# Two halves written out, with most of the modulation computed at the end of causal attention

## The chip, the cores and the metric

The kernel runs on one core of one Trainium2 chip, as one program. The metric is the device time of one execution in microseconds; of the kernel before there are three timed runs and one profiled execution. In the rows, PE is TensorE (PEld its weight loads), DVE VectorE, ACT ScalarE, POOL GpSimd and SP SyncE, which here only issues DMAs; a name with a q behind it is that engine's queue. Times are in us unless marked otherwise.

## The reference

Two transformer layers with adaptive layer norm, in float32, on x of 4 batches, 512 tokens and 512 features. Cut to what matters:

```python
mod = (silu(c) @ wmod).reshape(4, 6, 1, 512)            # per layer: sa, ca, ga, sb, cb, gb
ga = (2 * (ga >= 0) - 1) * maximum(abs(ga), 0.25)       # the gates; gb alike
h = layernorm(x) * (1 + ca) + sa
x = x + ga * causal_attention(h)    # layer 0: 32 query heads, 8 key/value heads of 128, rotary, wo
h = layernorm(x) * (1 + cb) + sb
x = x + gb * sign_ffn(h)            # sign(W), scaled by row_scale = mean|W| of a row, and scale_param
mod = (silu(c1) @ wmod1) ...        # layer 1, with its own c and wmod
x = x + ga * head_attention(h)      # layer 1: 32 heads of 16, attention among the heads of one token
x = x + gb * lora_experts(h)        # 8 experts of rank 16, the best one is chosen
```

`wmod0` and `wmod1` are 512 x 3072 each, 6 MB; one sixth of one of them, 512 x 512 and 1 MB, gives one of the six vectors per layer and is called a chunk here.

## The kernel before

**Stages.** Every stage is a block in which each engine has its own list of instructions, written out by hand and tied by semaphores; at its end stands a barrier of all engines (L81). A stage's work starts when the slowest engine, and the last DMA that SP waits for, are done.

1. `stage_modulation` (L90 to L203), once: SP loads both wmods in eight parts, PE multiplies silu(c) by them with the 4 batch columns as weights and 512 columns moving (L157), ACT takes the 4x512 rows out (L144), PE turns eight of the twelve into columns (L167) for `modT`, DVE makes the four gates (L190 to L196) and the mean of |W| (L182); gates and row_scale go to DRAM.
2. Then a loop on the device (`nc.Fori`) runs twice, over the two halves of the batches (2 batches, 1024 tokens each). In each pass: `stage_half_mod` copies this half's two columns of `modT` to `modh` (L497). `stage_norm` loads x and the gates (L370, L331), clears y, normalises batch by batch (statistics L413, Newton steps L433 to L436, `xn` L438), turns xn on PE (L459), applies scale and shift on ACT (L481), and splits the result, and the first group's weights, into a high part `hh` and a low part `hl` (L447, L392, L450; weights L534 and L538).
3. `stage_groups` (causal attention) runs once per half, in 64 steps, one for a query head and a batch; n counts them. Step n on PE: transposes of the probabilities (L732), the projection of a later query or key (L690), scores of head n + 1 (L715), `out_proj` for an earlier head pair (L771), and `weigh(n)`, probabilities times values (L753); ACT takes the product out (L876). The last steps have no projection. Behind step 63 stand four more output tiles. Weights come in eight groups; SP loads the next group's when POOL has split the last (L516, L521), and behind group 7 it loads group 0's again. `pj` is the PSUM bank most projections use; a projection waits until the bank's last one was taken by DVE.
4. `stage_middle`: residual, second norm, sign product, residual, third norm. `stage_qkv`: projections of layer 1, stored to DRAM in another order.
5. `stage_heads_and_finish` ("tail"): 16 pieces (`CHUNKS`) of attention among heads, whose first keys lie in the memory of y (`kd0`); gathers of the result by SP and ACT (L1468); output projection (L1526); last norm, experts (L1541, L1555); stores of x (L1491), for which SP waits.

## Time and profile before

| | us |
|---|---|
| timed runs | 2323.23, 2324.77, 2325.0 (median 2324.77) |
| the profiled execution, its own time | 2326.28 |
| span of its trace | 2324.4 |
| PE busy | 2038.9 |
| DVE, ACT, POOL busy | 1472.6, 1054.6, 1045.4 |
| mean granted clock of PE | 0.94 |

The span runs from the first to the last instruction in the trace; 1.9 us of the time lie around it. A row of a timeline gives start, duration, engine, line, operation, output and inputs, and in brackets how long the engine was idle before it and what ended that.

### The profile page before, as it was taken

To read this page: it belongs to the slowest core of one execution; us is meant where nothing else is said; L and a number is where in the kernel's file an instruction comes from. 1 tells how busy PE (TensorE), PEld (TensorE's weight loads), DVE (VectorE), ACT (ScalarE), POOL (GpSimd) and SP (SyncE) were. 2 spreads that over 40 slices of the span, in tenths; PEclk is the share of its full clock that TensorE was granted. 3 is DMA by queue.
4 is the path that set the end of the run, shared out by engine and by line. 5 is a ranking of instruction groups with operands and counts; after the bars stand their busy time and mean duration, and the time that the engine had idled before them with its cause. 6 is when DMAs were issued, how large, how long until landed. Compare 5 with 4: busy or idle time off the path is not lost. (4 is left out here: it accounts for less than half of the span.)

```text
span 2324.4 us, 34095 instructions
## 1 busy us (share of the span) xinstructions
PE 2038.9 (88%) x11760; PEld 1636.0 (70%) x11760; DVE 1472.6 (63%) x3703; ACT 1054.6 (45%) x2426; POOL 1045.4 (45%) x818
## 2 busy tenths in 40 slices
PE   7389999999999996587846999999999999964887
PEld 1278888888888885276525888888888888733664
DVE  1666666666666667833765666666666666676176
ACT  1255555555555553324214555555555555532232
POOL 0354555455555553343126545556455454435141
PEclk9599999999999998798977999999999999977989
DMA  6300000010000103025330001000010100030371
GB/s 250 118 19 28 19 28 19 28 46 19 28 19 28 46 19 120 12 73 118 70 128 28 19 28 46 19 28 19 28 39 13 41 19 28 19 132 28 94 128 47
DMA packets 129763, 118.55 MB, mean 51 GB/s; under 512 B 43172, under 2 KB 95396, under 8 KB 128564
## 3 DMA queue, kind: packets, MB, share of 16 engines
q1 hardware_dynamic: 121332, 107.07, 15.6%
q10 hardware_dynamic: 8256, 9.25, 1.4%
q8 instruction: 97, 1.59, 0.3%
q14 instruction: 78, 0.64, 0.1%
HBM read 95.29 MB, written 16.81 MB: 48 GB/s over the span
## 5 line engine op out<-in xcount | busy, mean ns | idle before, releaser
L996 POOL TENSOR_TENSOR gqa_rot<-gqa_rot,consts 128x512 f32<-128x512 f32 x160 | 209.4, 1309 | 641.9 <-ACT gqa_rot L817 641.8
L833 ACT ACTIVATE gqa_prob<-gqa_prob,gqa_nmax 128x128 f32<-128x128 f32 (+3 forms) x512 | 281.9, 552 | 198.5 <-DVE gqa_nmax L918 198.5
L918 DVE CUSTOM_DVE_ANT_0 gqa_prob<-gqa_pS,consts 128x128 f32<-128x128 f32 (+3 forms) x512 | 220.2, 486 | 73.8 <-PE gqa_pS L717 72.9
L926 DVE TENSOR_TENSOR gqa_ptl<-gqa_pT,gqa_pth 128x384 fp32r<-128x384 f32 (+1 forms) x384 | 218.2, 596 | 32.0 <-ACT gqa_pth L843 27.3
L843 ACT CAST gqa_pth<-gqa_pT 128x384 fp32r<-128x384 f32 (+1 forms) x384 | 182.5, 510 | 94.5 <-PE gqa_pT L732 94.5
L999 POOL TENSOR_TENSOR gqa_full<-gqa_full,gqa_rot 128x512 f32<-128x512 f32 x160 | 206.5, 1291 | 12.6
L771 PE MATMUL gqa_pW<-woh,gqa_oh 128*128 128x512 f32 x504 | 202.7, 402 | 9.0 <-DVE y L943 9.0
L690 PE MATMUL gqa_pj<-first_hh,wqh 128*128 128x512 f32 x496 | 205.7, 415 | 0.0
L771 PE MATMUL gqa_pW<-woh,gqa_ol 128*128 128x512 f32 x504 | 197.3, 392 | 0.0
L1008 POOL TENSOR_TENSOR gqa_ql<-gqa_full,gqa_qh 128x512 fp32r<-128x512 f32 x128 | 164.3, 1283 | 73.0 <-DVE gqa_qh L907 73.0
L771 PE MATMUL gqa_pW<-wol,gqa_oh 128*128 128x512 f32 x504 | 196.5, 390 | 0.0
L690 PE MATMUL gqa_pj<-first_hh,wql 128*128 128x512 f32 x496 | 194.5, 392 | 0.0
L690 PE MATMUL gqa_pj<-first_hl,wqh 128*128 128x512 f32 x496 | 193.6, 390 | 0.0
L715 PE MATMUL gqa_pS<-gqa_kh,gqa_qh 128*128 128x192 f32 (+3 forms) x512 | 172.5, 337 | 18.0 <-POOL gqa_ql L1008 17.7
L732 PE MATMUL gqa_pT<-consts,gqa_prob 128*128 128x128 f32 x1280 | 182.9, 274 | 2.1 <-DVE gqa_ptl L926 2.1
L876 ACT CAST gqa_oh<-gqa_pO 128x512 fp32r<-128x512 f32 x128 | 75.1, 587 | 239.7 <-PE gqa_pO L753 239.7
L732 PEld LDWEIGHTS gqa_pT<-consts,gqa_prob 128*128 128x128 f32 x1280 | 156.0, 141 | 36.1 <-DVE gqa_ptl L926 3.0
L935 DVE TENSOR_SCALAR gqa_prob<-gqa_prob,gqa_rden 128x128 f32<-128x128 f32 (+3 forms) x512 | 178.2, 411 | 4.5
L753 PE MATMUL gqa_pO<-gqa_pth,gqa_vh 128*128 128x512 f32 (+3 forms) x512 | 167.1, 326 | 14.7 <-DVE gqa_ptl L926 14.7
L943 DVE TENSOR_TENSOR y<-gqa_pW,y 128x512 f32<-128x512 f32 x252 | 171.7, 681 | 8.5 <-PE gqa_pW L771 5.6
L889 DVE SCALAR_TENSOR_TENSOR gqa_full<-gqa_pj,consts 128x512 f32<-128x512 f32 x156 | 107.4, 688 | 99.1 <-ACT gqa_rot L817 92.5
L717 PE MATMUL gqa_pS<-gqa_kh,gqa_ql 128*128 128x192 f32 (+3 forms) x512 | 165.7, 324 | 0.0
(245 smaller groups left out, 4866.8 us busy)
## 6 DMA issues: line engine op xcount, KB each, us to landing
raw_q<-in_wq SPq DMA_DIRECT2D x16, 1024.0 KB, 5.3
raw_o<-in_wo SPq DMA_DIRECT2D x16, 1024.0 KB, 5.2
mod_wm<-in_wmod SPq DMA_DIRECT2D x8, 1536.0 KB, 19.4
raw_kv<-in_wkv SPq DMA_DIRECT2D x16, 512.0 KB, 6.6
x<-in_x SPq DMA_DIRECT2D x4, 1024.0 KB, 6.4
kp<-qkv_rest SPq DMA_DIRECT2D x16, 256.0 KB, 2.3
qp<-qkv_rest SPq DMA_DIRECT2D x16, 256.0 KB, 2.3
vp<-qkv_rest SPq DMA_DIRECT2D x64, 64.0 KB, 1.8
```

Source lines behind the costliest of these rows:

```text
L690: mm = pe.matmul(bank[e][:], wp, hp[:, k, t], start=(n == 0), stop=(n == 3 * KT - 1))
L715: pe.matmul(out, qh[r][:, t], kh[u % 2][:, 0:wide], start=True, stop=False)
L732: mm = pe.transpose(pT[k % 2][:, c:c + P], prob[n % 2][:, P_OFF[i] + j * P:P_OFF[i] + (j + 1) * P], held.ident)
L771: mm = pe.matmul(wbank(d)[:], op[h % 4][:, t], wp[:, h % R0, :], start=(m == 0), stop=(m == 5))
L833: ins = nc.scalar.activation(p, p, ACT.Exp, scale=-1.0, bias=nmax[r][:, i:i + 1], accum_out=den[r][:, i:i + 1])
L843: nc.scalar.copy(pth[:, c:c + w], pT[k % 2][:, 0:w]).then_inc(pt_hi, 1)
L918: nc.vector.tensor_tensor_reduce(prob[r][:, P_OFF[i]:P_OFF[i] + w], pS[s][:, c:c + w], held.mask[:, T - w:T], -1.0, LARGEST, ALU.add, ALU.min,
L926: nc.vector.tensor_tensor(ptl[:, c:c + w], pT[k % 2][:, 0:w], pth[:, c:c + w].bitcast(F32), ALU.subtract).then_inc(pt_lo, 1)
L935: ins = nc.vector.tensor_scalar(p, p, rden[n % 2][:, i:i + 1], None, ALU.mult)
L943: nc.vector.tensor_tensor(y[:, j, :], wbank(d)[:], y[:, j, :], ALU.add).then_inc(w_added, 1)
L996: nc.gpsimd.tensor_tensor(rot[r % 2][:], rot[r % 2][:], held.sinT, ALU.mult).then_inc(sined, 1)
L999: nc.gpsimd.tensor_tensor(full[r % 2][:], full[r % 2][:], rot[r % 2][:], ALU.add).then_inc(roped, 1)
```

## The change

The loop over the halves is written out, so each stage exists twice, with constants where registers were; `stage_half_mod` and `modh`'s copy are gone (`modh` is a slice of `modT`). `stage_modulation` is gone. In `stage_first` of half 1, x and two chunks (shift and scale of the first norm) are loaded, PE computes the two between the two batches' transposes, with 128x128 pieces of wmod as weights and the 4 batch columns moving, so that columns come out directly. x lies in memory for half 2 already: it is loaded into y's memory in half 1's last stage, and x and y change places. y is cleared by POOL instead of DVE, and the Newton step has one operation less. raw_o is loaded in attention instead of in the norm.

The other ten chunks are computed in half 1's attention: nine behind `weigh(n)` of steps 55 to 63 and one behind step 63, each loaded by SP into the memory of raw_q when the chunk before is computed, each taken out by DVE. The gates, turned on PE, go to DRAM from there, and so does row_scale (`sign_scale`). Group 0's weights are no longer loaded and split behind group 7.

```diff
-def stage_modulation(nc, held, a):
...
-        with nc.Block() as block:
...
-                for l in range(2):
-                    for k in range(KT):
-                        pe.wait_ge(wm_in[l][k], 16)
-                        for i in range(NCH):
-                            if l and k == 0:
-                                pe.wait_ge(row_out, i + 1)
-                            mm = pe.matmul(pr[i][:], silu[:, k, l * B:(l + 1) * B], wm[l][:, k, i * D:(i + 1) * D],
-                                           start=(k == 0), stop=(k == KT - 1))
...
+def stage_first(nc, held, a, half, weights):
...
+            pM = [pT[HB * KT - 2 + i][:, 0:KT * B].rearrange("p (m b) -> p m b", b=B) for i in range(2)]
...
+                if half == 0:
+                    for l, c in enumerate((a["c0T"], a["c1T"])):
+                        sp.dma_start(cT[:, :, l * B:(l + 1) * B], c.rearrange("(k p) b -> p k b", p=P)).then_inc(c_in, 16)
+                    load_x(sp, 0)
+                    for i in range(2):
+                        sp.dma_start(wm[i][:], a["wmod0"][:, i * D:(i + 1) * D].rearrange("(k p) n -> p k n", p=P)).then_inc(wm_in[i], 16)
+                    load_x(sp, 1)
+                    rest = slice(0, 2 * T)
+                    sp.dma_start(held.consts[:, rest], a["tables"][:, rest]).then_inc(const_in, 16)
+                    sp.wait_ge(const_in, 16)
...
+                nc.gpsimd.memset(y[:], 0.0).then_inc(y_clear, 1)
+                def weight_los():
                     for n, (what, i) in enumerate(FIRST_PARTS):
                         pool.wait_ge(split_hi, n + 1)
                         weights.split_lo(what, i).then_inc(split_lo, 1)
-                if ahead:
-                    ahead.los(pool)
+
...
+                    v, h, r, t = var[:, s], half_var[:, s], rstd[:, s], step[:, s]
                     link(nc.vector.tensor_scalar(v, mv[:, s, 1], EPS, None, ALU.add))
+                    nc.vector.tensor_scalar(h, v, -0.5, None, ALU.mult)
...
-                        link(nc.vector.tensor_tensor(t, t, v, ALU.mult))
-                        link(nc.vector.tensor_scalar(t, t, -0.5, 1.5, ALU.mult, ALU.add))
-                        link(nc.vector.tensor_tensor(r, r, t, ALU.mult))
+                        link(nc.vector.tensor_tensor(t, t, h, ALU.mult))
+                        link(nc.vector.scalar_tensor_tensor(r, t, 1.5, r, ALU.add, ALU.mult))
...
+                normalise(0)
+                if half == 0:
+                    for ci in range(2):
+                        dve.wait_ge(mod_full, ci + 1)
+                        nc.vector.tensor_scalar(held.modT[:, 0, ci], pM[ci], float(ci), None, ALU.add).then_inc(mod_done, 1)
+                normalise(1)
...
+                turn(0)
+                if half == 0:
+                    for i in range(2):
+                        pe.wait_ge(wm_in[i], 16)
+                        for m in range(KT):
+                            for k in range(KT):
+                                mm = pe.matmul(pM[i][:, m, :], wm[i][:, k, m * P:(m + 1) * P], held.silu[:, k, 0:B],
+                                               start=(k == 0), stop=(k == KT - 1))
+                        mm.then_inc(mod_full, 1)
+                    pe.wait_ge(mod_done, 2)
+                turn(1)
...
+                if half == 0:
+                    ident = slice(2 * T, held.consts.shape[1])
+                    act.dma_start(held.consts[:, ident], a["tables"][:, ident]).then_inc(ident_in, 16)
+                    act.wait_ge(c_in, 32)
+                    nc.scalar.activation(ec[:], cT[:], ACT.Exp, scale=-1.0).then_inc(c_exp, 1)
+                    act.wait_ge(wm_in[0], 16)
+                weights.load_qkv(act, w_in, 0)
+
+                def weight_his():
+                    act.wait_ge(w_in, 32)
                     for what, i in FIRST_PARTS:
                         weights.split_hi(what, i).then_inc(split_hi, 1)
-                if ahead:
-                    ahead.load(act)
-                    for loaded in later:
...
-def stage_half_mod(nc, held, half):
...
-    for gr in range(GB):
+    for gr in range(GB - 1):
...
+LATER = [(0, 2), (0, 5), (1, 2), (1, 5), (0, 3), (0, 4), (1, 0), (1, 1), (1, 3), (1, 4)]
+NGATE = 4
+LATER_AT = 55
+STEP_OF = [0] * 4 + [n for n, step in enumerate(STEP_PROJ) for e in step]
...
+                wts.load_o(sp, wo_in, 0)
+                if later:
+                    sp.dma_start(sp_scale[:], a["scale_param"]).then_inc(sign_in, 16)
+                else:
+                    load_gates(sp, held, a, 0, half, gate_in)
+                for i in range(GB - 1):
                     if i:
                         sp.wait_ge(w_lo, last_split(("q", "kv"), i))
-                    wts.load_qkv(sp, qkv_in, after[i])
+                    wts.load_qkv(sp, qkv_in, i + 1)
                     sp.wait_ge(w_lo, last_split(("o",), i))
-                    wts.load_o(sp, wo_in, after[i])
+                    wts.load_o(sp, wo_in, i + 1)
+                sp.wait_ge(w_lo, last_split(("q", "kv"), GB - 1))
+                for j, (l, c) in enumerate(later):
+                    if j == 6:
+                        sp.wait_ge(w_lo, last_split(("o",), GB - 1))
+                        sp.dma_start(wts.raw_o[:], a["w_sign"].rearrange("(k p) n -> p k n", p=P)).then_inc(sign_in, 16)
+                    if j:
+                        sp.wait_ge(chunk_full, j)
+                    sp.dma_start(wts.raw_q[:], a["wmod0" if l == 0 else "wmod1"][:, c * D:(c + 1) * D].rearrange("(k p) n -> p k n", p=P)
+                                 ).then_inc(chunk_in, 16)
+                    if j == 6:
+                        sp.wait_ge(gate_left, 1)
+                        sp.dma_start(a["gates"].rearrange("g b (m p) -> (g b m) p", p=P), grow[:]).then_inc(rows_out, 16)
+                if later:
+                    sp.wait_ge(rows_out, 16)
+                    load_gates(sp, held, a, 0, half, gate_in)
+                    sp.wait_ge(scale_step, 3)
+                    sp.dma_start(a["row_scale"].rearrange("(k p) -> p k", p=P), row_scale[:], allow_slow_non_contiguous=True).then_inc(rows_out, 16)
+                    sp.wait_ge(rows_out, 32)
...
+                    if later and STEP_OF[e] > LATER_AT:
+                        pe.wait_ge(chunk_left, STEP_OF[e] - LATER_AT)
...
+                def modulate(j):
+
+                    n = LATER_AT + j
+                    free(max(e for e in range(len(PROJ)) if bank[e] is pj and STEP_OF[e] <= n))
+                    if j:
+                        pe.wait_ge(chunk_left, j)
+                    if j == NGATE:
+                        pe.wait_ge(gate_step, 5)
+                        pe.transpose(pj[0:NGATE * B * KT, T - P:], gT[:].rearrange("p g b m -> p (g b m)"), held.ident).then_inc(gate_turned, 1)
+                    pe.wait_ge(chunk_in, 16 * (j + 1))
+                    for m in range(KT):
+                        for k in range(KT):
+                            mm = pe.matmul(pj[:, m * B:(m + 1) * B], wts.raw_q[:, k, m * P:(m + 1) * P],
+                                           held.silu[:, k, later[j][0] * B:(later[j][0] + 1) * B], start=(k == 0), stop=(k == KT - 1))
+                    mm.then_inc(chunk_full, 1)
...
+                    if 0 <= n - LATER_AT < len(later):
+                        modulate(n - LATER_AT)
                     if n >= 2:
                         out_proj(2 * (n - 2) + 1)
+                for j in range(NH - LATER_AT, len(later)):
+                    modulate(j)
...
+                def modulation(j):
+
+                    l, c = later[j]
+                    dve.wait_ge(chunk_full, j + 1)
+                    got = pj[:, 0:KT * B].rearrange("p (m b) -> p m b", b=B)
+                    if j == NGATE:
+                        dve.wait_ge(gate_turned, 1)
+                        nc.vector.tensor_copy(grow[:], pj[0:NGATE * B * KT, T - P:]).then_inc(gate_left, 1)
+                    if j < NGATE:
+                        nc.vector.tensor_copy(gT[:, j].rearrange("p b m -> p m b"), got).then_inc(chunk_left, 1)
+                    else:
+                        ci = (0, 1, 3, 4).index(c)
+                        nc.vector.tensor_scalar(held.modT[:, l, ci], got, float(ci % 2), None, ALU.add).then_inc(chunk_left, 1)
+                    if j == NGATE - 1:
...
+                def sign_scale():
+
+                    dve.wait_ge(sign_in, 32)
+                    nc.vector.tensor_reduce(row_scale[:], wts.raw_o[:], AX.X, ALU.add, apply_absolute_value=True).then_inc(scale_step, 1)
...
+                for j in range(NH - LATER_AT, len(later)):
+                    modulation(j)
+                if later:
+                    sign_scale()
...
+                if half + 1 < B // HB:
+                    sp.wait_ge(s_full, CU * (UNITS1 - NK // 2))
+                    for b in range(HB):
+                        t0 = (half + 1) * HB * T + b * T
+                        sp.dma_start(held.y[:, b * TT:(b + 1) * TT, :], a["x"][t0:t0 + T, :].rearrange("(j p) d -> p j d", p=P)
+                                     ).then_inc(next_in, 16)
...
-        with nc.Fori(0, B // HB) as half:
-            stage_half_mod(nc, held, half)
+        for half in range(B // HB):
+            held.modh = held.modT[:, :, :, :, half * HB:(half + 1) * HB]
...
-                    stage_norm(nc, held, a, 0, 0, half, weights=wts)
-                    with nc.Fori(0, G // GB) as g:
-                        stage_groups(nc, held, a, wts, g * GB)
+                    wts = GroupWeights(gctx, nc, a, half)
+                    stage_first(nc, held, a, half, wts)
...
+            held.x, held.y = held.y, held.x
```

## Rows read from the trace of the kernel before

**Rows 1.** Profile page, busy time by engine over the span.
```profile
PE 2038.9 (88%) x11760; PEld 1636.0 (70%) x11760; DVE 1472.6 (63%) x3703; ACT 1054.6 (45%) x2426; POOL 1045.4 (45%) x818
```

**Rows 2.** Attention by stretch: us; busy PE, PEld, DVE, ACT, POOL; PEclk; DMA share; GB/s.
```profile
205.00:305.00 100.00, 98.57 (x529) 83.96 (x528) 66.68 (x179) 54.12 (x134) 51.38 (x40) 1.00 0.09 27
```

**Rows 3.** Timeline, modulation stage: start, duration, engine, line, output and input, count.
```profile
9.86 43.80 PE L157 MATMUL mod_pr<-mod_wm,mod_silu 128*4 128x512 f32 x96 [9.86 <-DMA mod_wm<-in_wmod]
...
38.71 2.29 DVE L182 TENSOR_REDUCE mod_rs<-mod_w 128x4 f32<-128x2048 f32 x1 [31.34 <-DMA mod_sp<-in_scale_param]
...
53.59 2.04 PEld L167 LDWEIGHTS mod_pc<-consts,mod_row 4*128 4x128 f32 x32 [0.86 <-issue]
```

**Rows 4.** Timeline, half-modulation copy, first norm and start of attention, half 1.
```profile
66.08 0.20 DVE L497 COPY modh<-modT 128x64 f32 x1 [3.01 <-PEq L81]
...
72.53 2.47 DVE L413 BATCH_NORM_STATS2 ln_stats<-x 128x6 f32<-128x512 f32 x4 [1.17 <-DMA x<-in_x]
...
78.31 1.92 DVE L438 TENSOR_SCALAR ln_xn<-x,ln_mv,ln_rstd 128x512 f32<-128x512 f32 x4
...
85.91 4.78 DVE L438 TENSOR_SCALAR ln_xn<-x,ln_mv,ln_rstd 128x512 f32<-128x512 f32 x4
...
104.26 0.76 PE L690 MATMUL gqa_pj<-first_hh,wkvh 128*128 128x512 f32 x1 [12.40 <-PEq L81]
```

**Rows 5.** Timeline of SyncE's DMA issues at the end of half 1.
```profile
1190.87 0.33 SPq L1491 DMA_DIRECT2D out<-x  x1
```

**Rows 6.** Timeline, from the last store of half 1 to half 2's norm.
```profile
1197.78 0.19 DVE L497 COPY modh<-modT 128x64 f32 x1 [8.43 <-issue]
...
1204.03 2.47 DVE L413 BATCH_NORM_STATS2 ln_stats<-x 128x6 f32<-128x512 f32 x4 [0.97 <-DMA x<-in_x]
...
1231.46 3.41 DVE L450 TENSOR_TENSOR first_hl<-ln_hf,first_hh 128x512 fp32r<-128x512 f32 x2
```

**Rows 7.** Timeline, a run of eight small products in the last stage.
```profile
1167.36 1.00 PEld L1541 LDWEIGHTS tail_pS<-lora_wA,tail_hf 128*128 128x128 f32 x8
```

**Rows 8.** The list of DMA issues from the trace, the output stores.
```profile
out<-x SPq DMA_DIRECT2D x16, 256.0 KB, 2.0
```

**Rows 9.** Timeline, end of attention and start of the middle stage.
```profile
901.79 0.47 PE L771 MATMUL gqa_pW<-woh,gqa_oh 128*128 128x512 f32 x1 [0.88 <-DVE y L943]
...
907.53 0.69 DVE L943 TENSOR_TENSOR y<-gqa_pO,y 128x512 f32<-128x512 f32 x1 [0.67 <-PE gqa_pO L771]
...
909.28 0.69 DVE L1115 TENSOR_TENSOR y<-y,gate 128x512 f32<-128x512 f32 x1 [1.06 <-PEq L81]
```

**Rows 10.** Timeline, GpSimd clearing a tile as large as y.
```profile
1007.14 3.53 POOL L1337 MEMSET y<- 128x4096 f32 x1
```

**Rows 11.** Profile page, DMA issues: transfer, count, size, median us to landing.
```profile
raw_q<-in_wq SPq DMA_DIRECT2D x16, 1024.0 KB, 5.3
```

**Rows 12.** Timeline, ScalarE taking each head's output, steps 54 and 55.
```profile
800.37 0.59 ACT L876 CAST gqa_oh<-gqa_pO 128x512 fp32r<-128x512 f32 x1 [1.31 <-PE gqa_pO L753]
...
811.02 0.59 ACT L876 CAST gqa_oh<-gqa_pO 128x512 fp32r<-128x512 f32 x1 [2.04 <-PE gqa_pO L753]
```

**Rows 13.** Timeline of SyncE's DMA issues, after the splits of step 54.
```profile
803.71 0.37 SPq L516 DMA_DIRECT2D raw_q<-in_wq  x1
```

**Rows 14.** Timeline, ScalarE taking the outputs of steps 62 and 63.
```profile
892.47 0.59 ACT L876 CAST gqa_oh<-gqa_pO 128x512 fp32r<-128x512 f32 x1 [2.65 <-PE gqa_pO L753]
...
899.54 0.59 ACT L876 CAST gqa_oh<-gqa_pO 128x512 fp32r<-128x512 f32 x1 [2.80 <-PE gqa_pO L753]
```

**Rows 15.** Timeline, PE after its idle time in half 1's last stage.
```profile
1183.69 0.69 PE L1549 MATMUL tail_pG<-consts,tail_wt 128*128 128x128 f32 x2 [4.28 <-DVE tail_wt L1745]
```

**Rows 16.** Table by stretch (columns as in Rows 2), the same place.
```profile
1182.00:1184.00 2.00, 0.31 (x2) 0.29 (x2) 1.50 (x7) 0.00 (x0) 0.39 (x1) 0.54 0.66 248
```

**Rows 17.** Timeline, last stage: SyncE's gathers.
```profile
1118.12 18.54 SPq L1468 DMA_DIRECT2D tail_at<-tail_o  x24
```

**Rows 18.** Timeline, last stage: PE's first output projections.
```profile
1130.52 10.57 PE L1526 MATMUL tail_pG<-out_w,tail_at 128*128 128x512 f32 x24
```

453 lines of the change are left out of this document (180 added, 273 removed).

## The prediction, made before the change was run

> **What bounds the kernel now.** I read the page's busy shares first: PE is busy for 88% of the span [rows 1]. A share over the whole span mixes stages, so the table by stretch came next. Inside causal attention, two stages of some 800 us each, PE is busy 98.57 of 100 us at a granted clock of 1.00 [rows 2], that is 2.4 GHz. Work put on PE there is paid in full; work on DVE (67%), ACT (54%) or POOL (51%) is not. Then I read the timelines of the places the change touches. In front of everything stands the modulation stage, where PE works through 96 records of 128x512 from 9.86 us for 43.8 us [rows 3]; the code has 48 matmuls there (2 layers, 4 k, 6 chunks), so **a float32 matmul makes two records**. DVE's gate and column work follows, and the next stage starts at 66.08 [rows 4]. The first norm's statistics start at 72.53 and the first attention matmul at 104.26 [rows 4]. So 104 us pass before the bound engine does work that bounds. Between the halves, the last store is issued at 1190.87 [rows 5] and the next norm's statistics start at 1204.03 [rows 6], with PE idle.
>
> **The change, part by part.** All times are from the profiled execution: span 2324.4, its own time 2326.3, which is 1.5 above the median of the runs shown (2324.8). I sum against 2326.3 and take the 1.5 off at the end.
>
> *Front of half 1.* The new first stage needs x's first MB, wmod0's first two chunks (1 MB each) and x's second MB, in this order on SP's queue. Transfer speed: the tables (0.8 MB) and the first wmod part (1.5 MB) had landed when PE started at 9.86 [rows 3], so with about 2 us to the first byte they moved at about 0.3 MB/us or better. Estimates: x's first MB by 7.5, chunk 1 by about 14, x's second MB by about 22, with attention's first weights on ScalarE's queue beside it. Statistics to xn took 78.31 - 72.53 = 5.8; the Newton step loses three linked operations of 0.2, so 5.3, and xn takes 1.92 [rows 4]: 14.7. PE's transposes end about 16. Then 2 chunks of 16 matmuls, 64 records. **Price of a record** of 128 weight columns and 4 moving columns: before has none. The nearest row is the transposition of 4-row slices, also 128 weight columns and 4 moving columns: 32 in 2.04 us, 0.064 each [rows 3]. The other end is a product with a full 128x128 weight tile and 136 moving columns: 8 in 1.00, 0.125 each [rows 7]. Less than 0.064 I exclude only down to 0.05, since nothing in the trace with 128 weight columns is quicker. I take 0.064, as the moving size is the same, and near twice that for part of the front, where PE has just begun: 6 us, to 22, and DVE's two additions to 22.5. The second norm: 2.5 + 2.9 on DVE, but now POOL works on hl and the weight splits beside it. Four tensor_scalars of xn took 4.78 beside POOL against 1.92 alone [rows 4]; I put 1.5 on Newton's four and take 4.8 for xn: 34. From the end of xn (85.91 + 4.78 = 90.69) to the first attention matmul passed 13.6 [rows 4]; ScalarE and POOL now have six splits each on that path or beside it, but POOL's end before the second half of it, so I take 12.5: attention starts at 46.5. Gain 104.3 - 46.5 = **57.8** (52 to 62).
>
> *Between the halves.* The last store lands 2.0 after its issue [rows 8], at 1192.9; with a barrier of 1.0 (DVE's last addition ends at 908.2, the next stage's first work stands at 909.3 [rows 9]) a stage that follows at once starts at 1193.9. Before, the copy of the half's modulation only started at 1197.78 [rows 6]: 3.9 for the loop's way back, which goes. The copy's own stage, the load of x and the clearing of y by DVE fill the rest to 1204.03, and go too, since x lies there and POOL clears y (3.53 [rows 10]). Sum 10.1. Inside the stage (1204.03 to 1234.87 [rows 6]) the Newton steps give 1.0, but weight splits on POOL now start some 5 us earlier and fall on the second Newton step: I take 1.5 net (-1 to 4). Gain **11.6**. The copy at 66.08 and its stage lie in the first term.
>
> *Loads in front of attention.* raw_o is loaded at the start of attention (5.3 [rows 11]) and needed at step 0's end, some 30 us on; in half 2 SP also waits for the gates before the next group's load, which has two steps of 10.7 us (811.02 - 800.37 [rows 12]) and more: 0. The last group's six splits per half go from ACT and POOL, which have slack: 0.
>
> *Ten chunks at the end of attention, half 1.* Each is 32 records at 0.064 = 2.05 on the engine that is busy all the time: 10 x 2.05 = **+20.5** (at 0.125: +40). Are their weights there in time? SP issued the load behind step 54's splits at 803.71 [rows 13], 1 MB takes 5.3 [rows 11], so 809.0; step 55's product ends at 810.8, just before ACT takes it [rows 12]. Cover 1.8, so chunk 0 waits for nothing. Chunks 1 to 7 are loaded from the end of the last chunk, with a step of 10.7 or more for 5.4. Chunk 8 has 7.1 (899.54 - 892.47 [rows 14]) plus its own 2: hidden. PE's waits added before projections (chunk_left) are met by a DVE copy that stands ahead of the addition, while PE runs an output projection of 1.4; behind such a wait the whole of PE would stand. **Chunk 9 has no step left.** Let T be the end of step 63's product, 899.4. Chunk 8 ends at T + 2.1, the load lands at T + 7.6, PE's only other work is one output projection (to T + 3.5). The last tiles, which began at 901.79 = T + 2.4 [rows 9], now start at T + 9.7: +7.3, of which 4.1 are the two chunks already counted, so **+3.2**. DVE then does sign_scale before the additions: the reduction of 2.29 [rows 3] and two small ones, 2.9, and PE's third tile waits for the first addition: **+1.0**. SP's gates and row_scale transfers end before the additions: 0. **Clock**: in half 1's last stage PE was idle for 4.28 before 1183.69 [rows 15], and the granted clock was 0.54 in 1182 to 1184 [rows 16], near 1.2 GHz. An idle stretch of 4.1 before chunk 9 is of that size. At 1.2 GHz the last chunk and some tiles take twice as long: **+2.5** (0 to 7).
>
> By the Trainium skill, "TensorE: Matmul & The Clock Gate", LDWEIGHTS, loading P weight columns takes P/1.2 ns, 107 ns for 128, whatever the rows. The row of 0.064 [rows 3] speaks against it; by the page the ten chunks would be 34 and the whole sum 14 us longer.
>
> *x for half 2 in the last stage.* SP issued its gathers from 1118.12 [rows 17]; the two x loads stand ahead of them, 1 us of issuing, and 2 MB ahead in the same queue, some 9 to 10 us. PE's first output projection was at 1130.52 [rows 18], so the first gather lands about then: **+0.5** (0 to 3).
>
> Sum: -57.8 - 11.6 + 20.5 + 3.2 + 1.0 + 2.5 + 0.5 = -41.7. 2326.3 - 41.7 = 2284.6, less 1.5: **2283**.
>
> **The rivals.**
> *Dense weights cost more.* If a record costs 0.107 to 0.125, the ten chunks take 34 to 40 instead of 20.5 and the front 1 to 2 more: 2298 to 2305. For it: the dense product's row [rows 7]; against: there the moving 136 columns may be what takes the time. Chance 0.25. This is also what the skill's rule gives.
> *Front shorter.* If POOL disturbs DVE less (xn 1.92, Newton undisturbed, casts short) and the clock stays at the end, 6 + 2.5 + 2 go: 2272. Chance 0.12.
> *PE's clock falls in steps 55 to 63.* A chunk is 2 us of records in which 4 columns move. If they count as idleness and the granted clock falls to 1.2 GHz for these steps, each microsecond is doubled: the 99 us from 800.37 to 899.54 [rows 12, 14] would cost 99 more, 2382, slower than before. It decides once more than 42 of these us run at the low level. Against it: over 8 of 10 us in each step are the same dense matmuls as now, at 1.00 [rows 2]. Chance 0.03.
> *The change brings nothing in front*, because the transfers, not PE's 96 records, set the start: then x or the chunks would arrive after 40 us. The tables and 1.5 MB had landed at 9.86 [rows 3], and 4.3 MB are needed: chance below 0.01.
>
> **How the numbers follow.** Likeliest (0.58): 2283, own range 2275 to 2292. Dense weights 0.25, front shorter 0.12, clock 0.03, the rest 0.02 is spread. The range reaches over the first three: 2270 to 2305. A measurement tells about 0.2% (4.6 us) from no change; only the clock rival and half of the rest are not faster: faster 0.96, same 0.01, slower 0.03.
>
> **What would show it.** In the profile after: first attention matmul at 46.5 (42 to 52); chunk records 2.05 a chunk in steps 55 to 63 and PE's share there still near 98%; PE idle 4 us before the last chunk, released by a DMA, with a clock near 0.5 behind it; attention of half 1 longer by 27; bn_stats of half 2 about 3 us after the last store's issue. Wrong would be: a chunk that waits for its weights in steps 55 to 62, 4 us a chunk instead of 2, or a first projection of half 1's last stage that waits for a gather by more than 3 us.

## The result, and the profile after the change

| | before | after |
|---|---|---|
| time, median (lowest to highest) | 2323.4 us (2321.0 to 2326.9, 20 runs) | 2328.5 us (2319.7 to 2334.9, 20 runs) |
| after over before | | 1.002, 95% interval 1.0013 to 1.0027 |
| the profiled execution: time, span | 2326.3, 2324.4 us | 2321.9, 2320.1 us |
| first attention matmul of half 1 | 104.26 | 55.06 |
| attention of half 1, to the middle stage's first work | 805.0 | 858.7 |
| from there to the first attention matmul of half 2 | 326.5 | 317.6 |
| the rest | 1088.6 | 1088.8 |

Forecast were 2283 us and a range of 2270 to 2305; the change brought nothing: after is some 5 us slower, 0.2%, and the interval lies just above 1. (The prediction knew three runs of before, with a median of 2324.8; the 20 runs have 2323.4.) The front gave 49.2 us and the boundary of the halves 8.9 (326.5 - 317.6), and the attention of half 1 took 53.7 of them back. The profiled execution of after lies 6.6 us below its own median, and after's runs spread over 15 us where before's spread over 6; that calls for an explanation too.

The page gives little away: PE is busy for 88% of a span that is 4 us shorter [against rows 1], and its clock line, tenths of full speed in 40 slices of 58 us, is lower in slices 15, 16 and 18 than before's. Lines of the page of after, and then the clock line of before:

```profile
PE 2048.0 (88%) x12017; PEld 1683.2 (73%) x12017; DVE 1463.7 (63%) x3696; ACT 1042.1 (45%) x2402; POOL 1035.3 (45%) x808
...
PEclk6999999999999987888978999999999999977989
```

```profile
PEclk9599999999999998798977999999999999977989
```

The timelines show where the time went. In front (start, duration, engine, line, output and input, count, idle time before and who ended it), the answer to [rows 4]:

```profile
15.10 3.65 PE L386 MATMUL ln_pT<-consts,ln_xn 128*128 128x128 f32 x16 [15.10 <-DVE ln_xn L356]
18.54 10.54 PE L399 MATMUL ln_pT<-silu,ln_wm 128*128 128x4 f32 x64
...
55.06 0.76 PE L623 MATMUL gqa_pj<-first_hh,wkvh 128*128 128x512 f32 x1 [6.70 <-PEq L81]
```

```profile
9.17 2.47 DVE L341 BATCH_NORM_STATS2 ln_stats<-x 128x6 f32<-128x512 f32 x4 [3.52 <-DMA x<-in_x]
...
32.67 0.16 DVE L352 TENSOR_TENSOR ln_step<-ln_rstd 128x4 f32<-128x4 f32 x1
32.87 1.18 DVE L353 TENSOR_TENSOR ln_step<-ln_step,ln_half_var 128x4 f32<-128x4 f32 x1
...
42.64 3.77 DVE L356 TENSOR_SCALAR ln_xn<-x,ln_mv,ln_rstd 128x512 f32<-128x512 f32 x4
```

The 64 records of two chunks took 10.54 us (0.165 each) where 6 were forecast. VectorE's small operations on 128x4 elements are 0.16 us long at 32.67 and 1.18 from 32.87 on, when GpSimd's subtractions run beside them (its first starts at 32.76).

The end of attention: PE's chunks (first, fourth, last), the matmul of an output tile behind the seventh chunk, and ScalarE taking the output of heads 53 and 63, which answers to [rows 12, 14]:

```profile
761.70 3.65 PE L720 MATMUL gqa_pj<-silu,raw_q 128*128 128x4 f32 x32
...
809.69 3.65 PE L720 MATMUL gqa_pj<-silu,raw_q 128*128 128x4 f32 x32
...
860.99 0.77 PE L704 MATMUL gqa_pW<-woh,gqa_oh 128*128 128x512 f32 x1
...
893.91 6.96 PE L720 MATMUL gqa_pj<-silu,raw_q 128*128 128x4 f32 x32 [3.76 <-DMA raw_q<-in_wmod]
```

```profile
737.08 0.59 ACT L830 CAST gqa_oh<-gqa_pO 128x512 fp32r<-128x512 f32 x1 [1.83 <-PE gqa_pO L686]
...
885.14 0.59 ACT L830 CAST gqa_oh<-gqa_pO 128x512 fp32r<-128x512 f32 x1 [2.82 <-PE gqa_pO L686]
```

A chunk takes 3.65 us, not 2.05; the next matmul starts 3.51 behind a chunk's first of 32 records, 0.110 a record. The output tile at 860.99 is at half pace (the next matmul of the same form follows 0.57 later and then every 0.43, where 0.23 is the distance at full clock). The granted clock was at its lower level there, 1.2 GHz, with PE busy all the time: the table by stretch of two such places (us; busy PE, PEld, DVE, ACT, POOL with counts; PEclk; DMA share; GB/s):

```profile
843.00:847.00 4.00, 4.00 (x14) 3.31 (x15) 0.60 (x2) 0.00 (x0) 0.00 (x0) 0.50 0.49 141
859.00:863.00 4.00, 4.00 (x17) 3.61 (x17) 0.17 (x1) 0.00 (x0) 0.30 (x1) 0.52 0.16 18
```

The last chunk waits 3.76 us for its weights and then takes 6.96 us. Behind it, VectorE's reduction, the store of row_scale and the middle stage's first work, the answer to [rows 9]:

```profile
901.00 2.27 DVE L926 TENSOR_REDUCE gqa_row_scale<-raw_o 128x4 f32<-128x2048 f32 x1
...
913.74 1.79 DVE L1108 TENSOR_TENSOR y<-y,gate 128x512 f32<-128x512 f32 x1 [5.23 <-PEq L81]
```

```profile
903.76 0.37 SPq L587 DMA_DIRECT2D row_scale<-gqa_row_scale  x1
913.71 0.38 SPq L102 DMA_DIRECT2D mid_hf<-in_w_signT  x1
```

```profile
row_scale<-gqa_row_scale SPq DMA_DIRECT2D x1, 2.0 KB, 8.9
```

VectorE stood idle for 5.23 us in front of the middle stage instead of 1.06: SyncE had issued the store of row_scale, 512 single 4-byte elements, at 903.76; it landed 8.9 us later, and the barrier follows.

**Split of the 53.7 us.** Until ScalarE takes head 53's output (786.2 before, 737.1 after) both kernels need the same time from the first attention matmul: 682.0 in both. In before:

```profile
786.22 0.59 ACT L876 CAST gqa_oh<-gqa_pO 128x512 fp32r<-128x512 f32 x1 [1.81 <-PE gqa_pO L753]
```

All of the difference lies behind it. From there to head 63's output (ten steps, called the ten steps from here on) there are 113.3 us before and 148.0 after (+34.7, eight chunks); from there to the last addition's start 8.0 and 22.7 (+14.7, two chunks and the reduction); from there to the middle stage 1.75 and 5.9 (+4.2). The table by stretch, before and then after, for the ten steps:

```profile
786.20:899.50 113.30, 108.60 (x589) 92.42 (x590) 75.31 (x199) 59.13 (x146) 52.24 (x41) 1.00 0.08 24
```

```profile
737.10:885.10 148.00, 145.36 (x847) 129.23 (x848) 78.03 (x213) 56.34 (x140) 44.37 (x35) 0.93 0.22 72
```

A mean granted clock of 0.93 over 148.0 us is a loss of some 10.4 us against full clock (an estimate, 148.0 x 0.07); without it the steps would have taken 137.6, so eight chunks cost 24.3, or 3.0 each. That is less than 8 x 3.51: PE was idle 4.7 us in before's ten steps and 2.6 in after's, and the rest of the difference is open. That gives the first theory: **work 24.3, clock 10.4, in the ten steps**. Its rivals: the loads or waits of the chunks, not their matmuls; and written-out code that runs slower than a loop.

### The profile page after: what moved, and what is told of

Read it like the earlier page. It is cut to its first block and busy times, and to the rows that moved or that the text cites. A ratio compares the mean times of both kernels' runs of the same rounds, so it can differ in the third digit from the quotient of the medians.

```text
span 2320.1 us, 34359 instructions
## 1 busy us (share of the span) xinstructions
PE 2048.0 (88%) x12017; PEld 1683.2 (73%) x12017; DVE 1463.7 (63%) x3696; ACT 1042.1 (45%) x2402; POOL 1035.3 (45%) x808
## 5 line engine op out<-in xcount | busy, mean ns | idle before, releaser
L992 POOL TENSOR_TENSOR gqa_full<-gqa_full,gqa_rot 128x512 f32<-128x512 f32 x160 | 206.6, 1291 | 12.6
L648 PE MATMUL gqa_pS<-gqa_kh,gqa_qh 128*128 128x192 f32 (+3 forms) x512 | 173.2, 338 | 16.4 <-POOL gqa_ql L1001 16.0
L686 PE MATMUL gqa_pO<-gqa_pth,gqa_vl 128*128 128x512 f32 (+3 forms) x512 | 165.6, 323 | 0.0
```

Of the source, the lines that this page charges most:

```text
L648: pe.matmul(out, qh[r][:, t], kh[u % 2][:, 0:wide], start=True, stop=False)
L686: mm = pe.matmul(pO[:, T - w:], vp[u % 2][:, v], pp[:, pc], start=(m == 0), stop=(m == 11))
L992: nc.gpsimd.tensor_tensor(full[r % 2][:], full[r % 2][:], rot[r % 2][:], ALU.add).then_inc(roped, 1)
```

## The experiments

Medians are compared with after's 2328.5. The kernel before was timed again beside each group of experiments, with medians of 2323.4 to 2325.0, so differences of 1 or 2 us between experiments say nothing. Each kernel is named by its label; the diffs are abridged.

**e1_one: the chunks' matmuls taken out.** Of 16 matmuls of a chunk one is left; the chunk values, and with them the gates and modulations, are not computed.

```diff
-for m in range(KT):
-    for k in range(KT):
-        mm = pe.matmul(pj[:, m*B:(m+1)*B], wts.raw_q[:, k, m*P:(m+1)*P], held.silu[...], ...)
+mm = pe.matmul(pj[:, 0:KT*B], wts.raw_q[:, 0, 0:P], held.ident[:, 0:KT*B], start=True, stop=True)
```

> Each of the ten chunks is computed with one matmul (2 records) instead of 16 (32 records); the other 15 are left out, so the ten chunks' values are not computed (gates and modulation come out wrong). Loads, evictions, waits and order stay. Theory A (the chunks cost what their records show in the changed kernel, 3.5 us each, and pull TensorE's clock down for a few us after each): 10 x 3.3 = 33 us fewer of work, and the windows with a granted clock of 0.5 to 0.9 behind each chunk vanish, another 7 to 12 us: 40 to 45 us below the changed kernel, 2283 to 2290. Theory B (the prediction's price of 2.05 us a chunk was right and the rest of the 53.7 us of the first attention lies elsewhere): 19 us less, about 2309, with the gap between two chunks still long. Theory C (the time of the chunks is that of their loads or evictions, not of the matmuls): less than 5 us.

Measured 2280.0 (2276.9 to 2281.6): 48.4 us below after (40.3 between the profiled executions, of which after's lay low). The ten steps take 115.4 us instead of 148.0, with the clock at 1.00:

```profile
740.50:855.90 115.40, 110.58 (x608) 94.29 (x608) 78.23 (x213) 56.11 (x141) 44.67 (x35) 1.00 0.28 92
```

So the chunks' matmuls, not their loads and waits (which are all still there), cost about as much as the front gains. Theories B and C fall; A's 40 to 45 was a little low. Whether it is their work or their clock this run does not part.

**e2_wide and e8_wide8: more columns beside the same weights.** The 4 moving columns are read 24 times (8 times in e8_wide8) with a step of zero; the result's first copy is used.

```diff
-mm = pe.matmul(pj[:, m*B:(m+1)*B], wts.raw_q[:, k, m*P:(m+1)*P], silu, ...)
+mm = pe.matmul(pj[:, m*24*B:(m+1)*24*B], wts.raw_q[:, k, m*P:(m+1)*P], silu.to_broadcast([P, 24, B]), ...)
```

> Each chunk matmul gets its 4 moving columns 24 times over (96 columns, read with a step of zero), so the same weights are loaded the same number of times and the results are the same; 24 times as many columns are streamed. Theory A (the record of 0.110 us is the load of the 128x128 weights, beside which 96 columns fit, and the clock falls behind a chunk because TensorE streams almost nothing during it): a chunk stays at 3.5 to 4.0 us at full clock, the windows at 0.5 to 0.9 behind the chunks vanish, and the kernel is 5 to 12 us faster than the changed one: 2316 to 2323. Theory B (the record's time goes by columns, or the clock falls for the gap that the weight loads leave whatever is streamed): a chunk takes 6 us or more, or the clock windows stay, and the kernel is 0 to 30 us slower than the changed one.

> The chunk matmuls with their 4 columns 8 times over (32 columns a record instead of 4; with 96 it was 14 us faster than the changed kernel, a chunk at 3.7 us and no fall of the clock before the last chunks). Theory A (the granted clock follows how many columns are streamed during the chunks): a part of the falls stays, 2 to 8 us faster than the changed kernel. Theory B (it is enough that the moving operand is not tiny): the whole 14 us. Theory C (the gain of the 96-column run came from the run's own luck with the clock): no difference from the changed kernel, 2326 to 2331.

Measured 2314.3 (2309.5 to 2319.2) with 96 columns and 2317.0 (2316.3 to 2318.7) with 32. A chunk of e2_wide, and the ten steps of e2_wide and of e8_wide8:

```profile
852.28 3.73 PE L722 MATMUL gqa_pj<-silu,raw_q 128*128 128x96 f32 x32
```

```profile
737.60:876.40 138.80, 135.78 (x848) 120.95 (x848) 77.56 (x213) 56.08 (x141) 44.41 (x35) 1.00 0.23 77
```

```profile
738.10:881.70 143.60, 140.55 (x849) 125.13 (x848) 77.81 (x213) 56.21 (x141) 44.40 (x35) 0.96 0.23 74
```

24 times as many columns cost 3.73 instead of 3.65 us, so the 0.110 us of a record do not go by its columns. Nor is 0.110 what any record costs: in before, records with weights of 32 columns and 68 moving columns start 0.049 apart (32 in 1.58), and transposes of full 128x128 tiles with 128 moving columns 0.110 (4 in 0.44), both at full clock:

```profile
1097.97 1.65 PE L1518 MATMUL tail_pO<-tail_bd,tail_pt 128*32 128x68 f32 x32
1099.55 1.08 PE L1504 MATMUL tail_pS<-y,tail_qq 64*32 64x128 f32 x32
...
1162.23 0.60 PE L1534 MATMUL tail_pO<-consts,tail_xn 128*128 128x128 f32 x4
1162.67 0.60 PE L1534 MATMUL tail_pG<-consts,tail_xn 128*128 128x128 f32 x4
```

What is left is that **a record's price is the load of its 128x128 weights**. And the clock does not fall any more in the ten steps: 1.00 with 96 columns, 0.96 with 32, 0.93 with 4. The same work became 14 us faster by streaming more, a little more than theory A's 5 to 12. With 32 columns the median is 11.5 lower, between theory A's part and theory B's whole; the runs of the two kernels overlap, so it is the clock in their profiles, and not the medians, that tells 32 columns from 96.

**e11_again: after itself, a second profile.**

> The changed kernel itself once more. Its profiled run (2321.9) lies 6.6 us below its median of 2328.5, and its runs spread over 15 us where those of before spread over 6. Theory A (the spread is the granted clock in steps 56 to 63): in a new profiled run the stretch from 740 to 900 us loses another amount than the 15 us of full-speed time of the first profile (each 20 us window's missing share of the clock, summed), and the run's time moves with it, by about half to the whole of the difference; the other stages stay within 1 us. Theory B (the spread comes from loads or from the start): the clock there is as in the first profile, and another stage carries the difference.

Measured 2329.1 (2321.6 to 2333.8); this profiled execution took 2333.7, 11.7 more than the first. Its ten steps:

```profile
740.20:893.00 152.80, 150.11 (x849) 133.09 (x848) 78.10 (x213) 56.49 (x140) 44.42 (x35) 0.90 0.21 70
```

The clock's loss is 15.3 instead of 10.4, and the steps take 4.8 more. But the other places are not within 1 us, as I had expected: the first attention matmul comes 3.1 later, since the two chunks in front took 13.65 instead of 10.54, and 2.4 and 1.8 are lost behind the attention. So of 11.7 us between the two executions the ten steps hold 4.8 and the front 3.1; the cause of the rest stays open. In five profiles with 4 columns (four kernels, after twice) the ten steps' length and the clock go together:

| kernel | ten steps, us | granted clock | loss, us | rest, us |
|---|---|---|---|---|
| after | 148.0 | 0.93 | 10.4 | 137.6 |
| e11_again | 152.8 | 0.90 | 15.3 | 137.5 |
| e3_pool | 152.9 | 0.90 | 15.3 | 137.6 |
| e7_front | 159.2 | 0.86 | 22.3 | 136.9 |
| e5_ends | 165.7 | 0.84 | 26.5 | 139.2 |
| e8_wide8 (32 columns) | 143.6 | 0.96 | 5.7 | 137.9 |
| e2_wide (96 columns) | 138.8 | 1.00 | 0 | 138.8 |

(Loss = length x (1 - clock), rest = length - loss.) **The rest is one number, 137 to 139; what differs is the clock.** Three more kernels with 96 columns, described below (e9_wide_ends, e6_all, e10_four), were at 0.99, and their ten steps took 142.5 each, with w_sign's sums inside them. So four profiles with 96 columns stand at 0.99 to 1.00 and five with 4 columns at 0.84 to 0.93.

**e5_ends and e9_wide_ends: the waits at the ends.** w_sign's sums and row_scale's store are put between chunks 6 and 8, chunk 9 goes into the buffer of wo beside chunk 8, and the next half's x is loaded behind the gathers: in e5_ends with 4 columns, in e9_wide_ends with 96.

```diff
+if j == 8:
+    sp.wait_ge(scale_step, 3)
+    sp.dma_start(a["row_scale"]..., row_scale[:], ...)
-if j:
+if j and j != 9:
     sp.wait_ge(chunk_full, j)
-sp.dma_start(wts.raw_q[:], ...)
+sp.dma_start(chunk_at(j)[:], ...)
...
+if later and n == LATER_AT + 6:
+    sign_scale()
-if later:
-    sign_scale()
```

> The changed kernel with its order at three places altered: the row sums of w_sign and the store of row_scale go in between chunk 6's eviction and chunk 8's load instead of behind chunk 9; chunk 9 is loaded beside chunk 8, into the buffer of wo's last group (free once w_sign's sums are done), instead of behind chunk 8's matmuls; the next half's x is loaded behind the last stage's gathers instead of in front of them. Theory A (these are waits on the path: 4.2 us at the start of the middle stage for row_scale, 3.8 us at chunk 9, 3.1 us at the last stage's first projection): the idle time before the middle stage's first work falls from 5.2 to about 1, chunk 9 takes 3.5 instead of 7.0 us, the projection's wait goes to 0, and about 2 us more come back because TensorE stays at full clock through chunk 9: 10 to 13 us below the changed kernel, 2315 to 2319. Theory B (each gives its place to the next wait: the gates' broadcast loads behind rows_out, the clock at the end of the attention, the gathers' own time): 0 to 4 us.

> The three edits of the ends (w_sign's sums and row_scale's store early, chunk 9 in a buffer of its own, the next half's x behind the gathers) on top of the chunks with 96 columns a record. With 4 columns a record the same three edits removed their waits in the trace and yet left the median where it was, with runs from 2316 to 2334. Theory A (the clock hid them: with 4 columns every few us of idle time gained go to a deeper fall of the clock in steps 56 to 63): here the clock is steady, so they count: 10 to 13 us below the 96-column run of 2314.3, at 2301 to 2305. Theory B (they are worth nothing on the path, and the later kernel with all edits owed its gain to its front and its second half): 2310 to 2315.

e5_ends: 2327.9 (2315.9 to 2334.2), no gain in the median; its mean, 2325.0, is 3.5 below after's, which is not clear of the noise. e9_wide_ends: 2301.7 (2299.9 to 2303.3), 12.6 below e2_wide, as theory A had it. The profiled executions are 6.2 apart, as e2_wide's lay 4.8 below its median; there, 3.8 us come from the middle stage's start and 6.7 from the end of attention, and 3.7 are given back in the ten steps, where the sums now stand. The waits did go in both. The first work of the middle stage and the last stage's first projection in e5_ends, and that projection in after:

```profile
926.11 1.79 DVE L1111 TENSOR_TENSOR y<-y,gate 128x512 f32<-128x512 f32 x1 [0.94 <-PEq L81]
...
1145.34 4.99 PE L1531 MATMUL tail_pG<-out_w,tail_at 128*128 128x512 f32 x11
```

```profile
1136.86 10.57 PE L1528 MATMUL tail_pG<-out_w,tail_at 128*128 128x512 f32 x24 [3.10 <-DMA tail_at<-tail_o]
```

Idle time of 0.94 instead of 5.23 us in front of the one, none instead of 3.10 in front of the other. In e5_ends' profiled run the ten steps took 17.7 more than in after's at a clock of 0.84, which ate all of it in that execution. Its runs lie in two groups, five at 2315.9 to 2318.4 and seven at 2326.9 to 2334.2, and the profiled one is of the upper group; no profile of the lower group was taken. Why its clock fell more than after's stays open; the order of the work in the steps before chunk 6 is the same.

**e3_pool and e7_front: VectorE beside GpSimd.** In e3_pool GpSimd waits with the weight parts until the second norm's Newton steps are done (in half 2 with all but two of them); e7_front does the weight parts of half 1 first, while VectorE waits for the two chunks.

```diff
 # e3_pool, GpSimd, half 1
+pool.wait_ge(newton, HB * (3 + 3 * NEWTON))
 # e7_front, ScalarE and GpSimd: the "if half:" goes from in front of weight_his() and weight_los()
-if half:
-    weight_los()
+weight_los()
```

> In the changed kernel GpSimd splits the first group's weights (six 128x512 subtractions) at the same time as VectorE works through the second norm's 18 small operations. Here GpSimd waits until those are done (in the second half after the first two parts). Theory A (the two engines take turns at a shared port, and each small operation waits out one of GpSimd's): the small operations fall from 1.18 us to about 0.16 to 0.25, 7 to 9 us in each half; GpSimd's own six subtractions then start later but end before the first group's projections need them, so the kernel is 10 to 18 us faster than the changed one: 2310 to 2318. Theory B (the small operations are slow for another reason, or the weight parts become the last thing the first projection waits for): 0 to 3 us, or the first projection waits for the weights' low parts by 5 us or more and the gain is gone.

> In the first half the six weight parts are rounded and split before the first norm's own tiles on ScalarE and GpSimd (as the changed kernel has it in the second half), so they run while TensorE works on the two chunks in front and VectorE waits, and not beside the second norm's small operations. Theory A (these operations run at 1.19 us beside a GpSimd subtraction and at 0.16 without one): only the four subtractions of the first image's low parts are left beside them, about 5 of the 9 slow operations become fast, 4 to 7 us less up to the first attention matmul. Theory B (the collision moves: the normalisation of 3.8 us or the casts slow down instead, as where GpSimd was made to wait and only 2.8 us of 9 came through): 0 to 3 us. The landing of wq's and wkv's first group at about 23 us is the mark to watch: beyond 29 it would delay the first image's tiles.

e3_pool: 2322.8 (2313.8 to 2326.0), 5.7 less, between theory A's 10 to 18 and theory B's 0 to 3; e7_front: 2329.8 (2316.6 to 2335.3), no gain in the median. VectorE in e3_pool:

```profile
32.87 0.16 DVE L358 SCALAR_TENSOR_TENSOR ln_rstd<-ln_step,ln_rstd 128x4 f32<-128x4 f32 x1
...
34.26 5.83 DVE L360 TENSOR_SCALAR ln_xn<-x,ln_mv,ln_rstd 128x512 f32<-128x512 f32 x4
...
42.11 4.82 DVE L378 CAST first_hh<-ln_hf 128x512 fp32r<-128x512 f32 x4 [2.02 <-ACT ln_hf L432]
```

Each small operation is back at 0.16 us and the Newton steps end 8.4 us earlier (34.26 instead of 42.64), but now xn takes 5.83 instead of 3.77 and the casts 4.82, since the same GpSimd work lies beside them: the first attention matmul comes at 52.27, 2.8 earlier, as theory B had it; between the halves 5.6 were left. e7_front moves the work where VectorE has nothing to do: 53.10, against 58.14 of e11_again, whose chunks in front took the same 13.65: 5.0, as theory A had it. Its median shows nothing of it, for the ten steps ran at 0.86.

**e4_unrolled: before, with its two loops written out.** Only the loop statements and the buffers' names change (for half in range(B // HB) instead of nc.Fori).

> The kernel before with its two loops (over the halves and over the groups of the last stage) written out, and nothing else changed. Theory A (the loop's way back costs the 3.9 us that the trace of before shows at the boundary, and nothing in the steps): 3 to 6 us faster than before, 2317 to 2320. Theory B (written-out code costs instruction loading in every step, more than the loops' way back saves): 0 to 10 us slower than before; the attention of the first half would then be longer than its 805.0 us by about as much.

Measured 2320.1 (2317.7 to 2322.5), 3.3 below before. The copy of the half's modulation, which in [rows 6] had 8.43 us of idle time before it:

```profile
1192.07 0.20 DVE L501 COPY modh<-modT 128x64 f32<-128x64 f32 x1 [4.53 <-PEq L85]
```

3.9 us less, and the attention of half 1 is as long as before's (804.1 us to 805.0). So the way back costs what was read from it, and code written out shows no cost of its own: the other rival falls.

**e6_all and e10_four: the better version.** e6_all has 96 columns, the three edits of the ends, the early weight parts and GpSimd's wait in half 2; e10_four also computes the second norm's two chunks in the front, one before and one behind the second image's transposes, and needs chunk 9's own buffer no more.

> All of these together: 96 columns a record in the chunks, w_sign's sums and row_scale's store early, chunk 9 in a buffer of its own, the next half's x behind the gathers, the weight parts early in the first half, and GpSimd waiting for the small operations in the second half. By the single runs: 14 (columns) + 10 to 13 (ends, less the 2 us that both count) + 4 (front) + 3 (second half) = 29 to 32 us below the changed kernel, 2296 to 2300. If each wait only makes room for the next: 2305 to 2314.

> The kernel of all edits (2292.9) with two of the ten chunks, the second norm's modulation, brought to the front: one in TensorE's idle time before the second image's transposes, one behind them, each beside work of VectorE and ScalarE; eight chunks stay in the attention, and w_sign's sums stay early. Theory A (TensorE is idle 10 us and 7 us there, and a chunk takes 3.7 to 6.8 us): the front stays within 1 us and the attention is 2 x 3.7 us shorter: 7 us below, 2285 to 2287; if TensorE also starts the projections at full pace because it was busy before them, another 2 to 4 us. Theory B (at the half pace of the front a chunk takes 6.8 us, and its 1 MB of loads comes in with the first group's): the front grows by 3 to 8 us and the kernel stays at 2290 to 2296.

e6_all: 2292.9 (2288.7 to 2296.3), ratio to before 0.986 (0.985 to 0.988), 3 us below the least that the single runs added up to. e10_four: **2288.2** (2286.6 to 2290.9), ratio 0.985 (0.983 to 0.987), 40 us below after, and between theory A's 2285 to 2287 and theory B's 2290 to 2296. The two ratios' intervals overlap, so that e10_four is the faster of the two is not shown. The front of e10_four, PE, and GpSimd's first weight part in e10_four and in e6_all:

```profile
18.79 10.54 PE L405 MATMUL ln_pT<-silu,ln_wm 128*128 128x4 f32 x64
...
34.56 6.96 PE L405 MATMUL ln_pT<-silu,ln_wm 128*128 128x4 f32 x32 [5.23 <-issue]
43.02 3.62 PE L394 MATMUL ln_pT<-consts,ln_xn 128*128 128x128 f32 x16 [1.50 <-DVE ln_xn L357]
...
46.47 3.73 PE L405 MATMUL ln_pT<-silu,ln_wm 128*128 128x4 f32 x32
...
53.43 0.77 PE L636 MATMUL gqa_pj<-first_hh,wkvh 128*128 128x512 f32 x1 [3.22 <-PEq L81]
```

```profile
29.26 1.27 POOL L255 TENSOR_TENSOR wkvl<-raw_kv,wkvh 128x512 fp32r<-128x512 f32 x1 [25.01 <-ACT wkvh L251]
```

```profile
24.24 1.27 POOL L255 TENSOR_TENSOR wkvl<-raw_kv,wkvh 128x512 fp32r<-128x512 f32 x1 [19.99 <-ACT wkvh L251]
```

Theory B holds for the front, where attention starts 3.4 later than in e6_all (50.07). The third chunk did run at half pace, 6.96, but the second image's transposes did not wait for it: it was done at 41.5, and they waited 1.50 more for VectorE's xn, which started at 42.42 instead of 39.12. Two more MB are loaded beside the first group's weights, and ScalarE got those at 28.6 instead of 23.5; so GpSimd's weight parts start 5 us later and fall on more of VectorE's small operations, the collision of e3_pool once more. Theory A holds for the end: from head 63's output to the last addition 8.0 us, as before the change, instead of 14.0.

## Why the prediction was wrong

The sum in the profiled execution should have been 2284.6 and was 2321.9: 37.3 us. The other 8.1 us between 2283 and 2328.5 are that the profiled execution of before was taken as 1.5 above its median and after's lay 6.6 below its own.

- **The price of a record, the step that failed.** The prediction had two rows, 0.064 [rows 3] and 0.125 [rows 7], and chose the first because its moving size was the same, 4 columns. The moving size did not matter: with 96 columns a chunk costs the same but for 0.08 us (e2_wide). The weights differed, 4 partitions deep in the row of 0.064 and full tiles of 128 partitions in the row of 0.125, and full tiles measured 0.110 at full clock. The row of 0.064 is also one of transposes, but transposes of full tiles start 0.110 apart as well; that the 4 partitions make it cheap is what is left, and no run changed them alone. By the Trainium skill, "TensorE: Matmul & The Clock Gate", LDWEIGHTS, 128 weight columns take 107 ns, and the prediction set this aside because of the row of 0.064; for full tiles this trace agrees with it (0.110), and for weights of 4 partitions the row still speaks against it. The 14 us that the prediction put on this rule left out the front's 64 records, some 3 us by the same figures (an estimate from the 107 ns of that page of the Trainium skill). Eight chunks cost 24.3 instead of 16.4: 7.9 of the 37.3.
- **The clock in steps 55 to 63, in the sum at nothing and a rival at 0.03; this step failed too, and by more.** The prediction argued that 8 of 10 us in a step are dense. That was no reason: the granted clock fell behind chunks (0.50 in 843 to 847, 0.52 in 859 to 863), for a few us, not for the whole of the steps. So the size of 99 us was wrong and so was the zero: 10.4 us in the profiled run and 15 to 27 in others. Of the 11.7 us between two executions of after, 4.8 lie in the ten steps. Why the clock fell: e2_wide and e8_wide8 change nothing but the number of streamed columns, and it rose with them.
- **The end of attention**: forecast +10.8 (two chunks 4.1, wait 3.2, sign_scale 1.0, clock 2.5), measured +14.7. The wait of chunk 9 was right (3.76 idle, released by the DMA), and the half clock behind it too; but at the true price of a record the chunk took 6.96 there.
- **row_scale: forecast 0, measured +4.2.** The prediction had the store end before the additions. It is issued behind the reduction, at 903.76, and landed 8.9 us later; the prediction gave 512 single elements of 4 bytes no time of their own. e5_ends and e9_wide_ends took the wait away.
- **Front: forecast 57.8, measured 49.2.** The second norm started at 29.2, not 22.5. Of these 6.7 us, 2.5 had passed before the chunks: x's first MB was there at 9.2, not 7.5, and the first transposes ended at 18.5, not 16. The chunks themselves took 10.5 instead of 6: the price of the record again, and the half pace from 22 us on, where the granted clock is 0.61 in 22 to 26 and 0.50 in 26 to 29. The second norm took 17.2 instead of 11.5: the collision of VectorE with GpSimd was put at 1.5 and is 8.4 in the Newton steps alone, 8 operations of 1.18 instead of 0.16. xn was put at 4.8 and took 3.8. From the end of xn to attention it was 8.65 instead of 12.5; the six splits, which the prediction had partly there, were done before. By the Trainium skill, "SBUF — State Buffer", Who interferes with whom, a VectorE instruction with two SBUF inputs contends with a GpSimd one that reads SBUF; the rows agree for the Newton steps. xn has one such input and slowed too, and so did two small tensor_scalars in half 2 (1.19 us at 1210.26, 1.12 at 1211.55); by the same section of the Trainium skill a tensor_scalar can enter modes that use the shared ports; no run here shows whether it did.
- **Boundary**: forecast 11.6, measured 10.0 from the last store's issue (1190.87 to 1235.82, now 1196.4, the end of the last group of issues less 0.3, to 1231.35). The way back was right (3.9 forecast, 3.9 in e4_unrolled), and so was the start of half 2's statistics, 3.25 us after the last store's issue; the Newton steps beside GpSimd took what is missing, and e3_pool got 5.6 back there.
- **x for half 2 in the last stage**: forecast 0.5, measured 1.1 from the middle stage's start to the last store's issue, though the first projection waited 3.10 for a gather, more than the 3 us that I had named as wrong.

In sum: 7.9 + 10.4 + 3.9 + 4.2 in attention, 8.6 in front, 2.2 behind the attention and 0.2 in the rest are the 37.3, but for rounding. The range lay wholly on the faster side: it took in the dearer record but gave the clock in the ten steps, row_scale's store and most of VectorE's collision with GpSimd nothing.

## What to carry to other kernels

Price a matmul by the weights that it loads and the columns that it streams, separately, and pick the row whose weights have the same shape; here a matrix times 4 columns was all weight load. When such matmuls go in between dense ones, look at the granted clock behind each of them, and stream more columns with the same weights if it falls: here that was worth 14 us for no work. And before a gain elsewhere is judged by a median, look whether the clock is steady: the same three edits gave nothing in the median where it fell, with runs 18 us apart, and 12.6 us where it held. When work is moved away from a collision, look what it lands on: in e3_pool 8.4 us were gained and 2.8 were left.

## What the runs showed of the hardware

- TensorE was busy 4.00 of 4.00 us in the stretches behind two chunks, and 145.4 of 148.0 over the ten steps, and its granted clock fell all the same: to 0.50 and 0.52 there, and to 0.84 to 0.93 over the ten steps with 4 columns a record, against 0.96 with 32 and 0.99 to 1.00 with 96.
- Reading an operand with a step of zero to make 4 columns 96 costs 0.08 us in a chunk of 3.65.
- The two chunks in front took 10.5 to 10.8 us (0.165 a record) in seven profiles and 13.65 or 13.66 (0.213) in four. In the second case that is half the pace of such records in the attention, and yet the granted clock is shown as 1.00 (22 to 26 us of e7_front); the clock column does not show this fall.

```profile
18.96 13.65 PE L396 MATMUL ln_pT<-silu,ln_wm 128*128 128x4 f32 x64
```

```profile
22.00:26.00 4.00, 4.00 (x20) 4.00 (x20) 0.17 (x1) 2.62 (x6) 1.92 (x2) 1.00 0.01 4
```

- A VectorE operation on 128x4 elements takes 0.16 us alone and 1.18 beside a GpSimd subtraction of 128x512; a tensor_scalar of 128x512 x4 takes 1.92 alone and 3.77 to 5.83 beside it. The store of 512 single elements of 4 bytes took 8.0 to 8.9 us from issue to landing in all eleven profiles of after and of the kernels made from it.
